# A time mix in sixteen chunks of 128 tokens, rewritten to work on four groups of 512 tokens

## What is computed

```python
xx = shifted(x) - x                                  # the token before, minus this one
mix = tanh((x + xx * maa_x) @ w1)                    # 5 x 32 low-rank columns
xw, xk, xv, xr, xg = (x + xx * (maa_s + mix_s @ w2_s) for s in five)
r, k, v, g = xr @ Wr, xk @ Wk, xv @ Wv, silu(xg @ Wg)
w = time_decay + tanh(xw @ dw1) @ dw2
for t in tokens:                                     # for each of 2 heads of 64
    y_t = r_t S + (r_t . (u * k_t)) v_t
    S = exp(-exp(w_t)) * S + k_t v_t^T
out = (groupnorm(y) * ln_w + ln_b) * g @ Wo
```

## Time and profile before

| | |
|---|---|
| median of 3 runs | 2161.71 us (2158.82 to 2162.98) |
| the profiled execution | 2161.64 us, of which the span of its instructions 2159.5 us |
| busy in the span: PE, DVE, ACT, POOL | 88%, 78%, 54%, 67% |
| first instruction of the time mix proper (xx, L449) | 9.37 us |
| last copy into `xa` (L392) | starts at 328.99 us, 0.27 us long |
| mean granted TensorE clock of the span | 0.919 of full |

### The profile page before, as it was taken

How to read it: one execution, slowest core, us unless ns; L and a number is a source line. 1 busy time by engine, 2 the same in 40 slices (tenths; PEclk the granted TensorE clock), 3 DMA queues, 4 the chain that set the end, 5 groups by cost and what they waited for, 6 DMA issues and landing times. The chain is left out here.

```text
span 2159.5 us, 87406 instructions
## 1 busy us (share of the span) xinstructions
PE 1890.9 (88%) x34160; PEld 1385.6 (64%) x34160; DVE 1694.1 (78%) x3442; ACT 1170.8 (54%) x2085; POOL 1457.0 (67%) x1150
## 2 busy tenths in 40 slices
PE   6776766899999999999999999999999999999995
PEld 4555543676666666666666676666666666666664
DVE  5777775888888888878788888888888878888874
ACT  1111113566656666666666666666666666656662
POOL 0000005888888887878787888888787878787871
PEclk6555557999999999999999999999999999999997
DMA  4000001222232222322222322223222223222220
GB/s 140 1 0 0 0 0 40 61 61 60 58 88 64 71 56 55 86 65 67 55 57 58 87 72 65 58 58 85 65 66 55 56 56 84 73 62 58 58 59 20
DMA packets 93565, 123.18 MB, mean 57 GB/s; under 512 B 27760, under 2 KB 41808, under 8 KB 93392
## 3 DMA queue, kind: packets, MB, share of 16 engines
q1 hardware_dynamic: 93232, 122.42, 22.5%
q10 hardware_dynamic: 288, 0.13, 0.0%
HBM read 20.74 MB, written 1.05 MB: 10 GB/s over the span
## 5 line engine op out<-in xcount | busy, mean ns | idle before, releaser
L886 POOL TENSOR_TENSOR across<-unit,turns 128x512 f32<-128x512 f32 x384 | 525.2, 1389 | 263.3 <-issue 252.3
L894 POOL TENSOR_TENSOR rotated<-along,across 128x1024 f32<-128x1024 f32 x192 | 496.2, 2584 | 20.4 <-POOL along L920 9.6
L1039 DVE TENSOR_REDUCE sums<-squares 128x16 f32<-128x1024 f32 x192 | 234.1, 1219 | 162.7 <-ACT squares L942 156.7
L1135 PE MATMUL turn<-identity,rotated 128*128 128x128 f32 x1536 | 204.2, 276 | 53.5 <-POOL rotated L894 53.5
L1135 PEld LDWEIGHTS turn<-identity,rotated 128*128 128x128 f32 x1536 | 172.1, 141 | 116.0 <-issue 101.1
L920 POOL TENSOR_TENSOR along<-unit,turns 128x1024 f32<-128x1024 f32 x96 | 227.6, 2371 | 0.0
L1240 PE MATMUL proj_a<-w_qkv,shift_a 128*128 128x512 f32 x384 | 189.5, 616 | 35.1 <-DVE unit L1064 25.4
L1001 ACT COPY val<-proj_a 128x1024 f32<-128x1024 f32 x96 | 97.2, 1012 | 179.6 <-PE proj_a L1240 179.6
L1265 PEld LDWEIGHTS att<-o_t,w_o 128*128 128x128 f32 x1536 | 188.2, 193 | 6.1 <-issue 1.0
L1168 PE MATMUL proj_a<-w_qkv,shift_a 128*128 128x512 f32 x384 | 185.7, 607 | 3.9 <-POOL shift_a L874 2.6
L1265 PE MATMUL att<-o_t,w_o 128*128 128x128 f32 x1536 | 188.6, 276 | 0.0
(11 more groups left out here) (183 smaller groups left out, 3783.2 us busy)
## 6 DMA issues: line engine op xcount, KB each, us to landing
v_win<-val SPq DMA_DIRECT2D x1536, 64.0 KB
w_qkv<-wqkv_dram SPq DMA_DIRECT2D x18, 512.0 KB, 3.9
w_o<-wo_dram SPq DMA_DIRECT2D x6, 512.0 KB, 4.3
where<-positions_dram SPq DMA_DIRECT2D x1, 2048.0 KB, 10.8
w_ffn<-ffn_dram SPq DMA_DIRECT2D x12, 170.5 KB, 2.3
w_ffn<-ffn_dram SPq DMA_DIRECT2D x6, 192.0 KB, 2.3
x_tok<-x_dram SPq DMA_DIRECT2D x4, 256.0 KB, 4.5
out_dram<-final SPq DMA_DIRECT2D x4, 256.0 KB, 2.4
```

What stands on the lines that cost most here:

```text
L886: pool.tensor_tensor(a[:, :, 1 - half, :], u[:, :, half, :], table, ALU.mult)\
L894: pool.tensor_tensor(rotated[j][:, :, :], along[j][:, :, :], across[j][:, :, :], ALU.add).then_inc(rotated_in[j], 1)
L1039: dve.tensor_reduce(sums[:, j, :], squares[j][:, :, :], AX.X, ALU.add).then_inc(summed[j], 1)
L1135: mm = pe.transpose(bank[:, TILE * (i % 4):TILE * (i % 4) + TILE], buffer[:, TILE * i:TILE * i + TILE], identity[:, :])
```

## The change

The chunks stay (state, masks and levels are per 128 tokens), but four of them are worked on by one instruction wherever that is possible: buffers are 512 wide (WIDE), and `step(m, g, e)` mixes group m, weighs group g and finishes group e. There are four groups, so `run` issues five steps and one more at the start, each written out; the hardware loop is gone. A step has at most one of each stage: step -1 mixes group 0, step 0 mixes 1 and weighs 0, steps 1 and 2 have all three, step 3 weighs 3 and finishes 2, step 4 finishes 3.

Further edits: the group's near blocks live in `proj_a` and `proj_b` (`near`, one bank for each head), and all of the mixing goes through two slots in `att` (`slots`), so the five streams are made one after another: `up(s)` on TensorE writes a slot, `stream(s)` on VectorE takes it (one scalar_tensor_tensor instead of share and shift_part), GpSimd adds x into `streams`. ScalarE, not VectorE, copies r, r with bonus and k out of PSUM. The mean and variance are taken by reduces and squares instead of bn_stats. `coef` holds only the 32 x 32 diagonal blocks; the far blocks stay in `far_32` and `far_64`, and y is built by small matmuls of 32 x 32, 64 x 64 and 32 x 32 parts of the array. The state has five buffers. GpSimd also multiplies the gate by the norm's weight and bias. TensorE sets x_one's transposes ahead of y.

The core of the diff, with the indentation shortened (first `run`, then GpSimd, ScalarE, VectorE, TensorE):

```diff
...
+CHUNKS_G = 4
+GROUPS = TILES // CHUNKS_G
+WIDE = CHUNKS_G * TILE
...
+    def near(c, h, at, size):
+    return nears[c // 2][:, h, 256 * (c % 2) + at:256 * (c % 2) + at + size]
...
+    step(i + 1 if i + 1 < GROUPS else None, i if 0 <= i < GROUPS else None, i - 1 if i >= 1 else None)
+
...
+                pool.wait_ge(s_part, MIXES * m + s + 1)
+                after(pool, s_gp, m)
+                pool.tensor_tensor(streams[:, s, :], shift_part[:, s, :], xb[:, group_cols(m)],
+                                   ALU.add).then_inc(s_stream, 1)
+        if e is not None:
+            pool.wait_ge(s_reps, e + 1)
...
+            act.wait_ge(s_kp, m + 1)
+            act.copy(kf[m % 2][:, :], slots[:, 1, :]).then_inc(s_k, 1)
+        if e is not None:
             act.wait_ge(s_yturn, e + 1)
+            after(act, s_out, e)
+            act.copy(y_t[:, :], turn[:, 1, :]).then_inc(s_yt, 1)
...
+            act.wait_ge(s_far, 2 * g + 2)
+            act.wait_ge(s_kturn, g + 1)
+            after(act, s_y, g)
+            for pair in range(2):
+                part = slice(4 * pair, 4 * pair + 4)
+                for q in (0, 2):
+                    rows = slice(WINDOW * q, WINDOW * q + WINDOW)
+                    act.copy(far_32[rows, part, :], by_head_chunk(pair)[rows, :, 0:WINDOW]).then_inc(s_far_kept, 1)
+                act.copy(far_64[:, part, :], by_head_chunk(pair)[0:64, :, 192:256]).then_inc(s_far_kept, 1)
+                act.copy(k_tok[:, 2 * pair:2 * pair + 2, :], nears[pair][:, :, 64:192]).then_inc(s_ktok, 1)
...
+    def scale_level(g, j):
...
+        dve.wait_ge(s_level, g * NEAR + j + 2 if j + 2 <= NEAR else (g + 1) * NEAR)
+        if j >= NEAR - 1:
+            dve.wait_ge(s_far, 2 * g + j - NEAR + 2)
...
+        def stream(s):
+            dve.wait_ge(s_up, MIXES * m + s + 1)
+            after(dve, s_stream, MIXES * (m - 1) + s + 1)
+            dve.scalar_tensor_tensor(shift_part[:, s, :], slots[:, s % 2, :], vec[:, V_MAA + s:V_MAA + s + 1],
+                                     xx[:, :], ALU.add, ALU.mult).then_inc(s_part, 1)
...
+        if g is not None:
+            scale_level(g, 0)
+        if e is not None:
+            dve.wait_ge(s_y, e + 1)
+            dve.tensor_reduce(y_sum[:, :], heads_of(turn[:, 0, :]), AX.X, ALU.add).then_inc(s_ysum, 1)
...
+        if e is not None:
+            dve.wait_ge(s_ysq, e + 1)
+            dve.tensor_reduce(y_var[:, :], y_sq[:, :, :], AX.X, ALU.add).then_inc(s_yvar, 1)
...
+        if g is not None:
+            scale_level(g, 2)
+        if m is not None:
+            stream(0)
+            stream(1)
+        if g is not None:
+            scale_level(g, 3)
...
+        if m is not None:
+            stream(2)
...
+        if m is not None:
+            stream(4)
+        if g is not None:
+            scale_level(g, 4)
+            dve.wait_ge(s_level, NEAR * (g + 1))
...
+            scale_level(g, 5)
+        if e is not None:
+            dve.wait_ge(s_out, e + 1)
+            dve.tensor_tensor(res[:, :, :], turn[:, 1, :].rearrange("p (c d) -> p c d", c=CHUNKS_G),
...
+        if g is not None:
+            dve.wait_ge(s_cut, 2 * g + 2)
+            after(dve, s_y, g)
+            for pair in range(2):
...
+        if g is not None:
+            dve.wait_ge(s_add, g + 1)
+            dve.wait_ge(s_scaled, 3 * LEVELS * (g + 1))
+            after(dve, s_y, g)
...
+        if e is not None:
             dve.wait_ge(s_pow2, e + 1)
+            dve.tensor_tensor(x_tok[:, CHUNKS_G * e:CHUNKS_G * e + CHUNKS_G, :], res_c[:, :, :],
...
+    def step(m, g, e):
+        def level(j):
+            source = rf_bonus[g % 2] if j == 0 else rf[g % 2]
+            for c in range(CHUNKS_G):
+                for q in range(BLOCKS):
+                    cols = slice(TILE * c + WINDOW * q, TILE * c + WINDOW * q + WINDOW)
+                    for h in range(R_HEADS):
+                        rows = slice(R_HEAD * h, R_HEAD * h + R_HEAD)
+                        mm = pe.matmul(near(c, h, WINDOW * j, WINDOW)[WINDOW * q:WINDOW * q + WINDOW, :],
+                                       kf[g % 2][rows, cols], source[rows, cols], start=True, stop=True)
+            mm.then_inc(s_level, 1)
+
+        def near_level(j):
+            pe.wait_ge(s_scaled, (g * LEVELS + j - 1) * 3)
+            level(j)
...
+                pe.wait_ge(s_part, MIXES * m + s - 1)
+            if s < 4:
+                mm = pe.matmul(slots[:, s % 2, :], w2_wide[:, s, :], mix[:, :], start=True, stop=True)
...
+        if g is not None:
+            pe.wait_ge(s_rb, g + 1)
+            pe.wait_ge(s_k, g + 1)
+            after(pe, s_state, R_HEADS * CHUNKS_G * g)
+            level(0)
+            level(1)
+        if m is not None:
             pe.wait_ge(s_xmix, m + 1)
...
+            pe.matmul(slots[:, 0, :], w1[:, 0:128], x_mixed[:, :], start=True, stop=True).then_inc(s_low, 1)
...
+            pe.matmul(slots[0:LORA, 1, :], w1[:, 128:160], x_mixed[:, :], start=True, stop=True).then_inc(s_low, 1)
+        if g is not None:
+            near_level(2)
+        if m is not None:
+            up(0)
+            up(1)
+        if g is not None:
+            near_level(3)
+        if m is not None:
+            up(2)
...
+        if g is not None:
+            near_level(4)
+        if m is not None:
+            up(4)
+            pe.wait_ge(s_stream, MIXES * m + 1)
...
+        if g is not None:
+            near_level(5)
+        if e is not None:
             pe.wait_ge(s_yg, e + 1)
...
+        if m is not None:
+            pe.wait_ge(s_stream, MIXES * m + 4)
+            pe.wait_ge(s_part, MIXES * m + 5)
+            pe.matmul(slots[:, 0, :], wr[:, 0, :], streams[:, 3, :], start=True, stop=True).then_inc(s_rp, 1)
+            pe.wait_ge(s_lora_t, m + 1)
+            pe.matmul(slots[:, 1, :], wr[:, 1, :], streams[:, 1, :], start=True, stop=True).then_inc(s_kp, 1)
+        if g is not None:
+            pe.wait_ge(s_scaled, (g * LEVELS + 5) * 3)
+            pe.wait_ge(s_cut, 2 * g + 2)
...
+        if e is not None:
             pe.wait_ge(s_yt, e + 1)
...
+        if m is not None:
+            pe.wait_ge(s_rb, m + 1)
+            tokens(0, 2, 2, s_vp)
+            pe.wait_ge(s_stream, MIXES * m + 5)
+            pe.wait_ge(s_k, m + 1)
+            tokens(1, 4, 3, s_gp)
+            pe.wait_ge(s_v, m + 1)
+            pe.matmul(slots[:, 0, :], dw2[:, :], low[:, :], start=True, stop=True).then_inc(s_rate_up, 1)
+        if g is not None:
+            pe.wait_ge(s_scaled, (g * LEVELS + 6) * 3)
...
+            pe.wait_ge(s_scaled, (g * LEVELS + 7) * 3)
+            for c in range(CHUNKS_G):
+                mm = pe.transpose(chunk_bank(c)[:, 64:192], kf[g % 2][:, TILE * c:TILE * c + TILE], identity[:, :])
+            mm.then_inc(s_kturn, 1)
+            pe.wait_ge(s_ktok, 2 * g + 2)
+            pe.wait_ge(s_far_kept, 6 * g + 6)
+            pe.wait_ge(s_v, g + 1)
+            for c in range(CHUNKS_G):
+                mm = pe.matmul(chunk_bank(c)[:, 288:416], k_tok[:, c, :], v_tok[g % 2][:, c, :],
+                               start=True, stop=True)
...
+        if e is not None:
+            pe.wait_ge(s_one, e + 1)
...
+        if g is not None:
+            pe.wait_ge(s_coef, 2 * g + 2)
+            after(pe, s_yc, g)
...
+                      slice(R_HEAD * h, R_HEAD * h + R_HEAD)) for c in range(CHUNKS_G) for h in range(R_HEADS)]
+            for c, h, out, part in sides:
+                for q in range(BLOCKS):
+                    rows = slice(WINDOW * q, WINDOW * q + WINDOW)
+                    mm = pe.matmul(turn[rows, 0, out], coef[rows, place(c, h), :], v_now[rows, c, part],
+                                   start=False, stop=False, skip_group_check=True)
+            mm.then_inc(s_ynear, 1)
+            for c, h, out, part in sides:
+                pe.matmul(turn[64:128, 0, out], far_64[:, place(c, h), :], v_now[0:64, c, part],
...
+            pe.wait_ge(s_ynear, g + 1)
+            for c, h, out, part in sides:
+                for q in (0, 2):
+                    rows = slice(WINDOW * q, WINDOW * q + WINDOW)
                     later = slice(WINDOW * q + WINDOW, WINDOW * q + 2 * WINDOW)
+                    mm = pe.matmul(turn[later, 0, out], far_32[rows, place(c, h), :], v_now[rows, c, part],
+                                   start=False, stop=True, skip_group_check=True)
...
```

More of the change, by code:

```diff
@@ L224, in time_mix @@
         norm_rows = sb("norm_rows", [128, 2, DIM])
[L225 to L254, removed]
-        y_b = sb("y_b", [128, DIM])
-        y_g = sb("y_g", [128, DIM])
@@ new lines, in time_mix @@
+        mix = sb("mix", [128, WIDE])
+        mix_last = sb("mix_last", [LORA, WIDE])
+        shift_part = sb("shift_part", [128, MIXES, WIDE])
+        streams = sb("streams", [128, MIXES, WIDE])
+        low = sb("low", [DECAY_LORA, WIDE])
+        rate = sb("rate", [128, WIDE])
+        decay_one = [sb(f"decay_one{i}", [128, WIDE]) for i in range(2)]
```

(20 more changed lines are left out.)

570 lines of the change are left out of this document (258 added, 312 removed).

## The result

The changed kernel takes **2054.38 us** (median of 4 runs, 2052.74 to 2057.84) where the kernel before takes 2162.35 us (2158.82 to 2163.13). The ratio is **0.9506, 95% interval 0.9489 to 0.9522**: 108 us less, where 92 were forecast (2069 us, range 2030 to 2107).

The account below looks back on a forecast made before the run. The time mix was taken as bound by a chain to and fro between PE and DVE, neither full. Steps of 21 + 45 + 108 + 35 + 18.5 = 227.5 us replace 319.9, 92.4 less: 2069 us, range 2030 to 2107.

Parts of the forecast that it names:

- Prices of wide work: Instruction prices: DVE on 512 columns 0.69 to 0.75 us, ACT 0.59 to 0.63, POOL 1.26, a level of 64 blocks 0.5.
- Parts of a full step: Eleven pieces followed along the waits (1, 3, 5 on DVE): sum 55.0 us, 54 with gaps, clock and POOL.
- Part 10: DVE's eight state updates, 2.5 us, and x_one, 0.7: 3.2 us, with PE waiting as x_one's transposes precede y.
- Part 11: PE: x_one's transposes 0.85, y 6.8, levels 0 and 1 1.0: 8.7 us, with nothing for DVE.
- Gaps, 7.4 us: Some 26 gaps of 0.25 us and nine hops of 0.1 between engines in a full step: 7.4 us.
- Parts 2, 4, 6 and 8: PE stretches (low matmuls, streams, levels, projections, far blocks, output) at the lower clock: 7.9, 3.9, 8.6 and 7.7 us.
- The clock, 10 us of a full step: PE bursts in parts 2, 6 to 8 and 11 lift the clock after 5 us: 10 us less a full step.
- POOL beside DVE, 1.5 us: POOL's stream additions slow DVE's two-operand instructions; on the chain only y_w and stream 3, 1.5 us a full step.
- Part 9, the reduces hidden: Level 6, k's transposes, ACT copies, state product: 6.2 us, with coef's two reduces of 1.45 us each lying under it.
- The rival of y's parts one after another: Near and far 32 take turns on one bank: 6.8 us a group, 27 in all, 2096 us; chance 0.10.
- The rival of a clock that stays low: The clock stays at its lower level, as in the kernel before: 2095 to 2110 us; chance 0.12.
- The rival of small blocks: The 544 small block instructions of a group don't overlap, some 100 us more a group, slower than before; chance 0.03.

Follow-up runs that it names:

- two_chunks: The changed kernel with groups of two chunks (256 columns) instead of four, nothing else: 2097.28 us, ratio to before 0.9732.
- coef_quarters: The changed kernel with coef's two reduces of 128 partitions each split into four of 32 partitions: 2086.94 us, ratio to before 0.9660.
- coef_early: The changed kernel with coef's two reduces ahead of level 6 on VectorE instead of behind res_c: 2052.33 us, ratio to before 0.9489.
- before_one_reduce: The kernel before with coef's four 32-partition reduces made one of 128, without placing on the diagonal blocks (y wrong): 2133.94 us, ratio 0.9874.
- xone_late: The changed kernel with x_one's transposes behind y on TensorE instead of ahead of it: 2044.90 us, ratio to before 0.9465.

## Why the prediction was right

- **What bounds, and that only the time mix moves:** right. Both engines' busy time fell, and they still take turns. How much of the gain is the width is shown from two chunks to four (39 us), not for the first doubling (two_chunks). The layers came out 2.2 us longer, which is within the scatter of the runs.
- **Prices of wide work:** right to a few per cent. A 128 x 512 operation of DVE took 0.68 to 0.75 us, L578 1.456 us (forecast 1.45). A level of 64 blocks took 0.64 to 0.83 us from its start to that of the next instruction (0.5): a small term, mis-sized by some 1 to 2 us a step. POOL's additions took 1.17 us (1.26).
- **Parts of a full step:** none off by more than 3 us. The errors have both signs, so it is in part luck that the full step is off by only 2.1 us (54 against 51.9). Parts 4 and 8 are short because their clock was 1.00 throughout (4.60 us busy in part 8, where the lower clock's price is 7.7). Part 10 is 0.9 us long because x_one took 1.58 us beside POOL's gate_b. Part 11 is 1.2 long.
- **Gaps, 7.4 us:** not settled. Parts 1, 3, 5 and 9 came out within 0.2 us of their prices without gaps. Parts 2, 4, 6 and 8 hide theirs behind the clock. An estimate from their windows: at clocks of 0.76, 1.00, 0.60 and 1.00, TensorE worked for 3.6 + 2.7 + 1.7 + 4.6 = 12.6 us at the higher level, and at the lower one the step would be at most that much longer. That is up to 64 us, against 62.4 forecast with gaps and 1.5 for POOL. So gaps of the forecast's size fit.
- **The clock, 10 us of a full step:** the mean came out (0.70 against 0.65 to 0.75), the gain may be some us larger than 10 by the estimate above, and the places were wrong. Part 11 has 8.4 us of PE without a break at 0.50, and I had it lifted after 5; part 8 was at 1.00 from its start. Step -1 was at 1.00 from the start, 17.8 us instead of 21.
- **POOL beside DVE, 1.5 us:** about the right size, in another place. y_w and stream 3 took 0.68 and 0.75, unharmed. y_g took 0.92 and x_one 1.58 instead of 0.69. TensorE waited for x_one, so 0.9 us are on the path; it did not wait for y_g.
- **Part 9, the reduces hidden:** right but for 0.6 us, and with no margin (coef_quarters, coef_early). For the kernel before, the prediction did not ask what its four reduces cost: up to 28.5 us of the time mix (before_one_reduce).
- **Part 10, TensorE's wait behind x_one:** right, and worth more than the 3.2 us of its work: 4.3 us of step 1 (xone_late). DVE's wait for TensorE in part 11, forecast as 8 us, was 7.3 and 10.0.
- **The rival of y's parts one after another:** refuted. Near took 1.93 us in each group, where 6.8 was the alternative. Its 64 instructions in four parts of the array took as long as far 32's 32 in two parts (1.92) and far 64's 16 in one (1.97), all into one bank. The Trainium skill, page TensorEngine Tiling (Array Packing), section Restrictions and Gotchas, would have different row tiles kept apart; no run here shows a cost for it, at either clock.
- **The rival of a clock that stays low:** wrong for the whole, right for part 11. **The rival of small blocks:** wrong, a level of 64 took 0.8 us at most.

The forecast was 14.6 us too high. In the time mix it is 13.2 (227.5 forecast, 214.3 measured): step -1 3.2, step 0 3.5, steps 1 and 2 2.1 and 3.6, step 4 0.9, while step 3 came out as forecast. Against that stand the layers with 2.2. The profiled execution of the changed kernel, 2057.84 us, is itself 3.5 above the median. What is still open is how much of each step's difference is gaps and how much is clock; no run takes the two apart.

## What to carry to other kernels

When two engines take turns and work is made wider, measure the changed kernel at a second width. It says how much of the gain is the width (39 us of 105.6 here) and gives a price of the step against a price of the chunk (9.5 and 10.6 us), though two widths can't test that line and the clock differs between them. Before counting an instruction's own time as the price of its place in the order, ask what it keeps waiting: xx and x_mixed were priced at 1.35 us, and their place held TensorE up for 3.85. And look for an instruction whose length goes by the free dimension only, and which is issued once for each quarter of the partitions; in the kernel before, that was worth up to 27 us.
